# Carried states in zero-padded 128x64 tiles, and the carry moved behind the first decay scan

## The reference

```
x = layernorm(x + ssm(x));  x = layernorm(x + mixture(x))

ssm:  z = x @ Wz;  ssm_in = x @ Win  ->  B, C (64 states), dt (8 heads), X (8 heads x 64)
      delta = softplus(dt + dt_bias)
      h_t = exp(-exp(A_log) * delta_t) * h_(t-1) + X_t (outer) (delta_t * B_t);  y_t = h_t . C_t
      y = y + D_param * X;   out = (y * (silu(z) @ Wzg)) @ Wout
mixture: three top-3-of-12 routers on x @ P_w; h = gelu(sum_e dw1[e] * (W1[e] @ x)); y = sum_e dw2[e] * (W2[e] @ h) + dw3 @ b2
```

## Time and profile before

| | |
|---|---|
| median of 3 runs | 1521.87 us (1521.78 to 1521.90) |
| the profiled execution's own time | 1522.09 us |
| its span in the trace | 1520.4 us |
| busy: PE, PE weight loads, DVE, ACT, POOL | 99%, 82%, 74%, 40%, 43% |
| granted TensorE clock | 0.999 |
| share of PE in the chain that ended last | 93% |

### The profile page before, as it was taken

One profiled execution on the slowest core, in us unless ns is written; L12 is line 12 of the kernel. 1 busy time (PEld: TensorE's weight loads), 2 busy tenths in 40 slices (PEclk: granted clock), 3 DMA queues, 4 the chain that ended last, 5 costly groups with the idle time before them and its releaser, 6 DMA issues.

```text
span 1520.4 us, 25377 instructions
## 1 busy us (share of the span) xinstructions
PE 1504.6 (99%) x8630; PEld 1250.7 (82%) x8630; DVE 1128.1 (74%) x3186; ACT 606.0 (40%) x1376; POOL 655.8 (43%) x747
## 2 busy tenths in 40 slices
PE   8999999999999999999999999999999999999998
PEld 7778888888888878888888888888888888888876
DVE  7797676967768677686876769777686776868755
ACT  6752424425244351533525244252443515335130
POOL 6771634616245270643606346162451715436040
PEclk9999999999999999999999999999999999999999
DMA  5350312314023040321404123140231403214020
GB/s 170 109 162 22 121 41 68 102 29 138 17 80 92 28 139 15 105 72 46 122 14 125 45 65 105 29 131 24 74 95 30 139 15 99 77 42 125 18 77 7
DMA packets 81505, 114.55 MB, mean 75 GB/s; under 512 B 10168, under 2 KB 37344, under 8 KB 81376
## 3 DMA queue, kind: packets, MB, share of 16 engines
q1 hardware_dynamic: 81376, 112.93, 24.6%
HBM read 107.77 MB, written 5.13 MB: 74 GB/s over the span
## 4 chain that ended last, share of the span: by engine, by line
PE 93%; POOL 2%; DVE 2%; DMA 1%; issue 1%; ACT 0%; SPq 0%; POOLq 0%; DVEq 0%; ACTq 0%
PE exp_bank L253 23%; PE exp_bank L255 22%; PE exp_bank L254 22%; PE mix_bank L964 4%; PE mix_bank L920 4%; PE mix_bank L253 3%; PE mix_bank L255 3%; PE mix_bank L254 3%; PE mix_bank L933 3%; PE mix_bank L814 1%; PE mix_bank L545 1%; PE mix_bank L762 1%; PE mix_bank L1056 1%; PE mix_bank L524 0%; POOL Wt L881 0%
## 5 line engine op out<-in xcount | busy, mean ns | idle before, releaser
L1241 POOL TENSOR_TENSOR sp_lo<-fbuf,sp_hi 128x512 fp32r<-128x512 f32 (+2 forms) x201 | 243.2, 1214 | 169.5 <-ACT sp_hi L1237 104.2
L253 PE MATMUL exp_bank<-w_hi,sp_hi 128*128 128x512 f32 x768 | 303.9, 396 | 1.2 <-POOL sp_lo L1294 0.8
L253 PE MATMUL exp_bank<-sp_hi,w_hi 128*128 128x512 f32 x764 | 302.8, 396 | 0.8 <-POOL sp_lo L1241 0.7
L255 PE MATMUL exp_bank<-w_hi,sp_lo 128*128 128x512 f32 x768 | 299.8, 390 | 0.0
L254 PE MATMUL exp_bank<-w_lo,sp_hi 128*128 128x512 f32 x768 | 299.0, 389 | 0.0
L255 PE MATMUL exp_bank<-sp_hi,w_lo 128*128 128x512 f32 x764 | 297.8, 390 | 0.0
L254 PE MATMUL exp_bank<-sp_lo,w_hi 128*128 128x512 f32 x764 | 297.5, 389 | 0.0
L1345 DVE SCALAR_TENSOR_TENSOR acc<-exp_bank,dw,acc 128x128 f32<-128x128 f32 x384 | 132.4, 345 | 163.6 <-PE exp_bank L255 162.8
L1237 ACT CAST sp_hi<-fbuf 128x512 fp32r<-128x512 f32 (+2 forms) x203 | 120.0, 592 | 270.7 <-DVE fbuf L1207 214.5
L881 POOL TENSOR_TENSOR Wt<-Wt,Gh 128x512 f32<-128x512 f32 x128 | 185.3, 1449 | 29.9 <-DVE Wt L870 29.9
L579 POOL TENSOR_TENSOR delta<-delta,bias_b 128x32 f32<-128x32 f32 x16 | 4.0, 253 | 414.3 <-ACT delta L555 409.2
(11 more groups left out here) (276 smaller groups left out, 2228.1 us busy)
## 6 DMA issues: line engine op xcount, KB each, us to landing
row_b<-dw_rows SPq DMA_DIRECT2D x189, 256.0 KB, 3.3
seg_b<-dA_rows SPq DMA_DIRECT2D x125, 256.0 KB, 3.4
ctd<-cum_rows SPq DMA_DIRECT2D x128, 96.0 KB, 3.2
x_in<-in_x SPq DMA_DIRECT2D x16, 256.0 KB, 2.7
result<-acc SPq DMA_DIRECT2D x15, 256.0 KB, 2.2
fbuf<-in_W1T SPq DMA_DIRECT2D x12, 256.0 KB, 4.0
acc<-in_W2T SPq DMA_DIRECT2D x4, 256.0 KB, 3.5
x_in<-in_W2T SPq DMA_DIRECT2D x4, 256.0 KB, 2.8
```

The source lines that it names most:

```text
L253: nc.tensor.matmul(ps, s_hi, m_hi, start=start and j == 0, stop=False, skip_group_check=onto)
L255: last = nc.tensor.matmul(ps, s_lo, m_hi, start=False, stop=stop and j == n - 1, skip_group_check=onto)
L1241: sig("xw_lo", on.tensor_tensor(lo[:, cols], wide[e % 2][:, cols], hi[:, cols].bitcast(F32), ALU.subtract))
```

## The change

The carried products use the same tile shape as the within-chunk products. For this the state of a pair of heads lies twice in a padded tile of 128 partitions: head j's state on its own 64 partitions, zeros on the other 64 (`S_wide` for the states of chunks 1 and 2, laid over `xT_hi` and `xT_lo`; `S_last`, in the old `S`, for chunk 3). POOL zeroes `S_wide` in each batch (`S_zero`). The first state is copied out of PSUM by ACT, in two halves (`state_0`), where DVE did it. The carry steps move on DVE into `mix_carry`, behind `mix_decay(0)`: one multiply straight from PSUM, then two adds, two multiplies and two adds on 64 partitions each. Batch 0 keeps the old form. Lines of the diff with `wait` are waits on the semaphores above.

```diff
--- before.py
+++ after.py
@@ -40,13 +40,13 @@
     + [(f"z{k}", "silu", k + 1) for k in range(NK)]
     + [(f"X{c}", "Xd", c + 1) for c in range(2)] + [("G", "Gm", 1), ("rates", "ends", 1), ("X2", "Xd", 3)]
     + [(f"zg{q}", "zg", q + 1) for q in range(NQ)]
-    + [("X3", "Xd", 4), ("st01", "state", 2), ("st2", "state", 3)]
+    + [("X3", "Xd", 4), ("st01", "state", 1), ("st2", "state", 2)]
     + [(f"y{q}", "gated", q + 1) for q in range(NQ)]
     + [("out", "v", 1), ("lg", "lg", 1)]
 )
 MIX_USE = {u[0]: n for n, u in enumerate(MIX_USES)}
 MIX_FIRST = (
-    MIX_USES[:MIX_USE["X2"] + 1] + [("X3", "Xd", 4), ("st01", "state", 2), ("st2", "state", 3)]
+    MIX_USES[:MIX_USE["X2"] + 1] + [("X3", "Xd", 4), ("st01", "state", 1), ("st2", "state", 2)]
     + MIX_USES[MIX_USE["st2"] + 1:]
 )
 START_BANK = {(0, f"zg{q}"): q for q in range(4)}
@@ -109,7 +109,9 @@
 
         x_in = sb("x_in", [P, NC, D])
         xT = sb("xT", [P, T])
+        halves_at = nc.sbuf_base
         xT_hi, xT_lo = sb("xT_hi", [P, T], F32R), sb("xT_lo", [P, T], F32R)
+        S_wide = nc.alloc_sbuf_tensor_at("S_wide", [P, 2, 2, NQ * HD], F32, offset=halves_at)
         BT, CT = sb("BT", [P, T]), sb("CT", [P, T])
         B_tok = sb("B_tok", [P, NC, NS])
         Xd = sb("Xd", [P, NC, DI])
@@ -117,6 +119,8 @@
         Gh = [sb(f"Gh{n}", [P, NC, P]) for n in range(2)]
         Wt = sb("Wt", [P, 2, 2 * T])
         S, St = sb("S", [P, NC - 1, NQ * HD]), sb("St", [P, NQ * HD])
+        S_last = S[:, 1:NC - 1, :]
+        S_pad = [S_wide[:, 0], S_wide[:, 1], S_last]
         pw, ut = S[0:P_w.shape[0], 0, 0:D], S[0:P_w.shape[0], 0, D:2 * D]
         ctd = sb("ctd", [P, 2, T - P])
         dA_t, cum_t = sb("dA_t", [P, P]), sb("cum_t", [P, P])
@@ -182,7 +186,7 @@
             ps_xT=1, xT=1, xT_lo=1, ps_dtB=1, dt_raw=1, dt_v=15, dt_s=2, dt_q=1, a_split=1, ps_BC=1, BC=1,
             ps_z=NK, tanh=NK, silu=NK, silu_hi=NK, silu_lo=NK, ps_X=NC, Xd=NC, ps_zg=NQ, zg=NQ,
             ps_dA=1, dA=1, ecum=1, ps_G=1, Gm=1, ps_ends=1, end_sum=1, ends=1, end_dt=1, Xde=NC - 1,
-            ps_st=2, state=NC - 1, st_tmp=NC - 2, ctd=NQ, scan=H, G_dt=H, W=H,
+            ps_st=2, state_0=1, state=NC - 2, st_tmp=NC - 2, ctd=NQ, scan=H, G_dt=H, W=H,
             ps_yw=NQ, ps_ys=NQ, gated=NQ, ps_out=1, v=1,
 
             ln1_v=7, ln1_s=2, x1=1, ps_x1T=1, x1T=1, ps_lg=1, lg=1, rt_v=8, rt_s=1, dw=1, ps_dwT=1, dwT=1, dw3T=1, dw3=2,
@@ -192,6 +196,7 @@
         ).items():
             product(name, n)
         product("G_skip", H, 1, 1)
+        product("S_zero", 1, 1, 1)
         product("xw", E, less=2)
         product("xw_hi", E + 1, less=1)
         product("xw_lo", E + 1, less=1)
@@ -527,6 +532,8 @@
                 wait(AC, "ps_xT", b)
 
                 wait(AC, "ps_X" if early else "ps_yw", b.prev())
+                if not early:
+                    wait(AC, "ps_ys", b.prev())
                 if 0 in parts:
                     AC.copy(xT_hi[:, :], bank_of("xT", b)[:, :])
                 if 1 in parts:
@@ -815,20 +822,62 @@
                                          B_tok[:, c, :], xv[:, j], start=True, stop=True)
                     if c > 0:
                         sig("ps_st", last)
-            if eng is DVE:
+            if eng is PO and not first(b):
+                wait(PO, "ps_X", b)
+                if b.reg is None and b.off == 1:
+                    wait(PO, "ps_ys", b.prev())
+                    PO.memset(S_last, 0.0)
+                sig("S_zero", PO.memset(S_wide[:, :, :, :], 0.0))
+            if eng is AC and not first(b):
+                wait(AC, "ps_st", b, 1)
+                wait(AC, "S_zero", b)
+                wait(AC, "ps_ys", b.prev())
+                for j in range(2):
+                    n = slice(j * NS, (j + 1) * NS)
+                    copied = AC.copy(S_pad[0][n, j, :], bank_of("st01", b)[n, 0:N])
+                sig("state_0", copied)
+            if eng is DVE and first(b):
                 for c, (use, at, k) in enumerate(place):
                     ps = bank_of(use, b)[:, at:at + N]
                     wait(DVE, "ps_st", b, k)
-                    wait(DVE, "ps_ys", b.prev())
                     if c == 0:
-                        sig("state", DVE.tensor_copy(S[:, 0, :], ps))
+                        sig("state_0", DVE.tensor_copy(S[:, 0, :], ps))
+                        wait(DVE, "state_0", b)
                     else:
-                        wait(DVE, "state", b, c)
-                        sig("st_tmp", DVE.tensor_tensor(
-                            St[:, :].rearrange("p (q n) -> p q n", n=HD), S[:, c - 1, :].rearrange("p (q n) -> p q n", n=HD),
-                            total[:, c * NQ:(c + 1) * NQ].unsqueeze(2).to_broadcast([P, NQ, HD]), ALU.mult))
+                        wait(DVE, "state", b, c - 1)
+                        sig("st_tmp", DVE.tensor_tensor(groups(St[:, :]), groups(S[:, c - 1, :]), total_of(c), ALU.mult))
                         wait(DVE, "st_tmp", b, c)
                         sig("state", DVE.tensor_tensor(S[:, c, :], St[:, :], ps, ALU.add))
+
+        def groups(v):
+            return v.rearrange("p (q n) -> p q n", n=HD)
+
+        def total_of(c, n=slice(0, P)):
+            return total[n, c * NQ:(c + 1) * NQ].unsqueeze(2).to_broadcast([n.stop - n.start, NQ, HD])
+
+        def mix_carry(eng, b):
+
+            N = NQ * HD
+            rows_of = [slice(j * NS, (j + 1) * NS) for j in range(2)]
+            if eng is DVE:
+                wait(DVE, "state_0", b)
+                wait(DVE, "S_zero", b)
+                wait(DVE, "ps_ys", b.prev())
+                ps0, ps1 = bank_of("st01", b)[:, 0:N], bank_of("st01", b)[:, N:2 * N]
+                sig("st_tmp", DVE.tensor_tensor(groups(St[:, :]), groups(ps0), total_of(1), ALU.mult))
+                wait(DVE, "st_tmp", b, 1)
+                for j, n in enumerate(rows_of):
+                    last = DVE.tensor_tensor(S_pad[1][n, j, :], St[n, :], ps1[n, :], ALU.add)
+                sig("state", last)
+                wait(DVE, "state", b, 1)
+                for j, n in enumerate(rows_of):
+                    last = DVE.tensor_tensor(groups(St[n, :]), groups(S_pad[1][n, j, :]), total_of(2, n), ALU.mult)
+                sig("st_tmp", last)
+                wait(DVE, "ps_st", b, 2)
+                wait(DVE, "st_tmp", b, 2)
+                for j, n in enumerate(rows_of):
+                    last = DVE.tensor_tensor(S_pad[2][n, j, :], St[n, :], bank_of("st2", b)[n, 0:N], ALU.add)
+                sig("state", last)
 
         def mix_score_step(eng, b, h):
 
@@ -924,13 +973,17 @@
         def mix_y_carried(b, q, opens):
 
             ps = mix_bank(b, f"y{q}") if opens else bank_of(f"y{q}", b)
+            wait(PE, "state_0", b)
             wait(PE, "state", b)
             wait(PE, "ctd", b, q + 1)
             alone(PE)
+            if not first(b):
+                wait(PE, "S_zero", b)
             for c in range(1, NC):
                 for j in range(2):
-                    n = slice(j * NS, (j + 1) * NS)
-                    last = PE.matmul(ps[j * HD:(j + 1) * HD, tok(c)], S[n, c - 1, q * HD:(q + 1) * HD],
+                    n = slice(j * NS, (j + 1) * NS) if first(b) else slice(0, P)
+                    state = (S[n, c - 1] if first(b) else S_pad[c - 1][:, j])[:, q * HD:(q + 1) * HD]
+                    last = PE.matmul(ps[j * HD:(j + 1) * HD, tok(c)], state,
                                      ctd[n, q % 2, (c - 1) * P:c * P], start=opens and c == 1, stop=not opens and c == NC - 1)
             sig("ps_ys", last)
 
@@ -1423,15 +1476,16 @@
                     wait(SP, "xw", p, 3)
                 load_w(eng, [N1 + 5, N1 + 6])
                 ahead = [6]
-            mix_states(eng, b)
             if norm_before or eng is not AC:
                 mix_score_step(eng, b, 0)
+            mix_states(eng, b)
             if not norm_before:
                 expert_prep(eng, p, 5)
                 load_w(eng, [N1 + 7])
             experts(eng, p, [2], ahead)
             mix_score_skip(eng, b, 0)
             mix_decay(eng, b, 0)
+            mix_carry(eng, b)
             if norm_before or eng is not AC:
                 mix_score_step(eng, b, 1)
             e = 3
```

## The result

| | before | after |
|---|---|---|
| median | 1521.82 us (6 runs, 1521.27 to 1522.00) | 1567.77 us (6 runs, 1565.65 to 1572.16) |
| profiled execution: own time, span | 1522.09, 1520.4 us | 1572.16, 1570.4 us |
| granted TensorE clock | 0.999 | 0.986 |
| ratio, with its 95% interval | | 1.0308 [1.0293, 1.0323] |

The change costs 46 us, 3.1%. The forecast had the sign and the first mechanism, but its 1543 is 25 us short, and 1567.77 lies outside its range.

A forecast was written before the change was run, and what follows sets the result against it. TensorE, busy 99% of the span, was taken as the bound. Batches 2 to 15 at 14 x (1.82 - 0.28) = 21.6 and batch 1 at -0.28 gave +21.3 us: 1543 us, range 1528 to 1547.

The forecast's parts named there:

- the first mechanism: DVE's later carry delays expert 5's input by 2.11 us, past a slack of 0.40, so TensorE waits.
- The seams (Part 1): TensorE's carried and within blocks merge, saving a 0.14 us shape change in each of two pairs: 4.2 us in all.
- The lock (Part 3): A middle carry multiply on DVE stands still until POOL's multiply of head 0 is over: carry grows by 1.04 us.
- the rival: DVE's middle carry multiplies get through before POOL's multiply of head 0: 1529 to 1533 us, chance 0.22.
- The price of the halves: DVE's carry instructions on 64 partitions cost as much as whole ones, making the seven-instruction carry 2.74 us.
- what a wait costs: TensorE's stall ahead of expert 5: 1.71 us of waiting plus 0.11 for the new start, 1.82 a batch.
- batch 1, one input further ahead: -0.28: In batch 1 expert inputs are one further ahead, hiding the lateness; only the seams' gain counts: -0.28 us.
- the slack: Time between expert 5's input being ready and TensorE starting expert 5 in the kernel before: 0.40 us in batch 8.

The follow-up runs named there:

- e5: Kernel after, zeros ahead of POOL's expert 2 part, DVE carrying unpadded states right behind the state sums, ACT copying all three into padded tiles: 1518.62 us, 0.9978.
- e6: As e5, but each carried product reads only its own 64 partitions (64x64 tiles, as in before): 1522.39 us, 1.0003.
- e8: Kernel after, with POOL's multiply of head 0 moved behind its low part of expert 5: 1567.44 us, 1.0299.
- e7: Kernel before, with only its five DVE carry instructions moved behind the first scan, old tiles, no zeros: 1539.70 us, 1.0115.
- e4: Kernel after, zeros ahead of POOL's expert 2 part, carry straight behind the state sums, ACT's copies behind its PSUM reads: 1528.15 us, 1.0040.
- e1: Kernel after, with eight unread 128x128 identity matmuls on TensorE ahead of expert 5 in batches 2 to 15: 1556.37 us, 1.0227.
- e9: Kernel after, with batch 1's zeros alone moved ahead of expert 2's input: 1564.17 us, one execution.
- e10: Kernel after, with batch 1's carry alone moved behind expert 6's multiply: 1563.19 us, one execution.
- e2: Kernel after, with the carry moved straight behind the state sums, ahead of expert 4's multiply: 1579.99 us, 1.0378.
- e11: Kernel after, with four unread 128x128 matmuls instead of eight ahead of expert 5 in batches 2 to 15: 1557.08 us, one execution.
- e3: Kernel after, with the carry moved behind expert 6's multiply: 1539.85 us, 1.0118.

## Why the prediction was wrong

**The seams (Part 1): right.** 0.15 for each of two pairs of blocks and 3.8 us by e5 against e6, for 0.14 and 4.2. The padded products cost nothing: the Trainium skill (TensorEngine Tiling (Array Packing), When to Use Tiling) would have them tiled by rows for speed; e5 and e6 do not agree with that here, where the shape of the neighbours counts for more. What the same page states under Key Properties, that a change of tiling mode drains TensorE, agrees with the 0.15.

**The lock (Part 3): right, 1.00 for 1.04.** 1.85 against 0.85 for the middle pair, ending 0.28 behind POOL, in the kernel after and by its absence in e8; the same 1.00 in e7. That the number fits is in part luck. POOL's multiply starts 5.63 behind the state sums and not 5.43, and takes 1.53 for 1.29; DVE's first half gets in 0.04 ahead of it, as the rival had it. But POOL's multiply slips in ahead of the second half, so the rival's time did not come.

**The price of the halves: mis-sized.** "Halves on 64 partitions are taken at the price of whole ones" took the second half 0.34 behind the first, as independent instructions of whole width are in the earlier trace rows. It follows after 0.43, and so does the whole-width instruction behind a second half: four places x 0.09 make 3.10 of the 2.74 (e4 shows 3.19, with one gap of 0.10 besides). Expert 5 is late by 2.29 to 2.34 in an undisturbed body and not by 2.11, and a body costs 1.71 for 1.54. The Trainium skill (VectorE: DVE Perf Modes, Two Vector instructions with no wait between them) states that an instruction whose operands start in another group of partitions than those of the last one starts only when that is finished. By that rule, the trace agrees: here the second half starts 0.01 behind the end of the first, where the earlier trace rows have an overlap of 0.08. The prediction did not weigh it. This term is 2.4 us of the 28.7 missing.

**The step that failed: what a wait costs.** "TensorE waits 1.71, and 0.11 for the new start, 1.82 us" priced the stall at its length. A stall by which expert 5 starts 1.9 us late is also followed, in 9 of 14 bodies, by 3.4 us at 1.2 GHz, which cost 1.85 more. This is 16.7 us of the profiled execution, and e1 gets 11.4 back on the median by giving TensorE something to do. No body of before has a wait of that length, so no row there priced it; but no bound was taken for it either, and the range should have had one.

**Batch 1: wrong.** The term "batch 1, one input further ahead: -0.28" took the carry's lateness as hidden there; batch 1 costs +7.2, of which 2.3 are its falls of the clock. The lead of one expert is 2.72 us, the lateness 4.7. The step did not look at POOL's queue in batch 1, where the splitting of weights stands ahead of the zeros, and DVE now waits for them. The late rows and the doubled fall are 2.5 us; the late rows are the same mistake in small: the slack that the stall used up had other users.

Together 2.4 + 16.7 + 7.2 + 0.28 + 2.5, less 0.3 at the two ends, are the 28.7 us between 21.3 and the 50.0 of the profiled spans, but for 0.1 of rounding. The median lies 4.4 below that execution. e9 and e10 leave batches 2 to 15 as they are in the kernel after, and each has six falls there instead of nine; three falls fewer are 5.6 us, about that difference.

**Open.** Why nine waits brought a fall and five of nearly the same length didn't. In the profiled execution of after the five start expert 5 at 11.63 to 11.68 and the nine at 11.69 to 12.90, but in e9 starts at 11.99 and 13.02 have none and several at 11.89 have one, so the length of the wait alone doesn't decide. In e2, where TensorE waits 2.4 us ahead of expert 4 in ten of batches 2 to 15, four of the ten bodies have a fall and six have none. Waits of 0.6 to 1.5 us, in e7, had none.

## What to carry to other kernels

A stall of the bounding engine is priced at its length and at what it does to that engine's clock; where no row shows a wait of that length, put a bound on it, and if a wait can't be avoided, a few matmuls that nobody reads are cheaper than the fall (e1). Before an order is changed, follow each new wait through the queue of every engine in every form of the loop body, the first batch too. And leave the layout work (padding, copying) to an engine with pauses, so that the engine whose queue feeds the bound one keeps its few full-width instructions: that turned 3.1% slower into 0.22% faster.

## What the runs showed of the hardware

- A single wait of 1.8 to 2.9 us in a stream that is otherwise 99% busy brought the granted clock from 2.4 to 1.2 GHz for 3.4 us, once for 6.8, in 9 of 14 bodies of the kernel after; four 128x128 matmuls in the wait kept it at 2.4 GHz in 13 of 14 bodies (e11, one execution), eight in all (e1).
- Independent DVE instructions of 256 columns on partitions 0 to 63 and 64 to 127 in turn follow each other after 0.43 us; two on all 128 partitions followed after 0.34.
- Of two DVE multiplies in a row that each read two SBUF operands, the first ran in 0.42 us while POOL's multiply came in, and the second stood still until 0.28 us behind POOL's end. In e3, where POOL has no pause, both stood still, for 0.35 and 1.00 us.
